# Gated cross-attention layer on one core: the first two projection jobs share one pass over half of the tokens

## The reference, cut to what matters

```python
x = x + tanh(g_xattn) * xattn(layernorm(x), ctx)      # x, ctx: 8 sequences x 128 tokens x 512
x = x + tanh(g_ffn)   * ffn(layernorm(x))

def xattn(hidden, ctx):            # H = 32 heads of DH = 128
    h_q = rmsnorm(hidden) @ w_q.T
    h_k = ctx @ w_k.T
    h_v = ctx @ w_v.T
    score = softmax(mask(h_q @ h_k.T + position_bias))
    return hidden + (score @ h_v) @ w_out.T
# ffn: a linear layer, a router over 15 entries and a low-rank update
```

## Time and profile before

| | |
|---|---|
| three runs | 832.13 us median (831.62 to 833.58) |
| the profiled execution | 832.1 us, span of the core 830.3 us |
| PE busy | 821.9 us (99%) |
| DVE busy | 491.8 us (59%) |
| ACT busy | 429.9 us (52%) |
| POOL busy | 348.3 us (42%) |
| the chain that ended last | 95% PE, 3% DVE, 1% DMA |
| PE's first instruction to first product of job 0 | 1.46 us to 6.75 us |
| `m1(2)` begins | 29.78 us |
| `m1(3)` begins | 36.66 us |

### The profile page before, as it was taken

One profiled execution on the slowest core, in us unless ns is written; L12 is line 12 of the kernel. 1 busy time (PEld: TensorE's weight loads), 2 busy tenths in 40 slices (PEclk: granted clock), 3 DMA queues, 4 the chain that ended last, 5 costly groups with the idle time before them and its releaser, 6 DMA issues.

```text
span 830.3 us, 13268 instructions
## 1 busy us (share of the span) xinstructions
PE 821.9 (99%) x4200; PEld 699.7 (84%) x4200; DVE 491.8 (59%) x919; ACT 429.9 (52%) x1065; POOL 348.3 (42%) x223
## 2 busy tenths in 40 slices
PE   8999999999999999999999999999999999999998
PEld 7888888888888888888888888888888888888876
DVE  6766666673353435555666565556655655677875
ACT  6667776676676665544444444444444444444320
POOL 0354544664556551434443344344434434432332
PEclk9999999999999999999999999999999999999999
DMA  8655555568555565766665566665666566655002
GB/s 307 199 170 151 163 158 153 165 183 268 173 163 161 173 201 161 241 193 195 188 190 193 190 198 203 203 202 177 187 193 175 178 191 188 216 166 160 32 26 77
DMA packets 147486, 147.60 MB, mean 178 GB/s; under 512 B 10992, under 2 KB 109936, under 8 KB 147056
## 3 DMA queue, kind: packets, MB, share of 16 engines
q1 hardware_dynamic: 147440, 147.02, 58.5%
HBM read 94.55 MB, written 52.43 MB: 177 GB/s over the span
## 4 chain that ended last, share of the span: by engine, by line
PE 95%; DVE 3%; DMA 1%; issue 1%; ACT 0%; SPq 0%; DVEq 0%
PE Sb L1528 7%; PE Ab L1539 7%; PE Sb L1359 7%; PE Sb L1361 7%; PE Sb L1360 7%; PE Vb L1350 4%; PE Vb L1351 4%; PE Vb L1352 4%; PE Kb L1350 4%; PE Kb L1351 4%; PE Kb L1352 4%; PE Ob L1350 4%; PE Ob L1351 4%; PE Ob L1352 4%; PE Ab L1361 3%; PE Ab L1359 3%
## 5 line engine op out<-in xcount | busy, mean ns | idle before, releaser
L536 POOL TENSOR_TENSOR bm<-bias,maskneg 128x512 f32<-128x512 f32 x64 | 83.6, 1306 | 178.6 <-DVE s_sb L1075 178.6
L756 ACT ACTIVATE p_exp<-s_sb,negmax 128x128 f32<-128x128 f32 x256 | 99.8, 391 | 76.5 <-DVE negmax L1077 76.5
L499 POOL TENSOR_TENSOR w_lo<-w_raw,w_hi 128x1280 fp32r<-128x1280 f32 (+1 forms) x29 | 87.0, 2999 | 116.4 <-ACT w_hi L626 116.4
L626 ACT ACTIVATE A_hi<-Ab 128x512 fp32r<-128x512 f32 x64 | 38.3, 598 | 164.0 <-PE Ab L1539 164.0
L1075 DVE TENSOR_TENSOR s_sb<-Sb,bm 128x512 f32<-128x512 f32 x62 | 42.8, 690 | 121.6 <-PE Sb L1528 121.6
L626 ACT ACTIVATE U<-Sb 128x512 f32<-128x512 f32 x90 | 53.9, 599 | 64.4 <-PE Sb L1361 64.0
L527 POOL TENSOR_TENSOR o_lo<-o_raw,o_hi 128x512 fp32r<-128x512 f32 x32 | 52.5, 1639 | 45.0 <-ACT o_hi L626 45.0
L626 ACT ACTIVATE w_hi<-w_raw 128x512 fp32r<-128x512 f32 (+3 forms) x68 | 60.1, 889 | 21.4 <-PE Kb L1361 8.2
L1539 PEld LDWEIGHTS Ab<-pT,V 128*128 128x128 f32 x512 | 66.9, 191 | 5.0
L1359 PE MATMUL Sb<-t_hi,w_lo 128*128 128x512 f32 x180 | 70.1, 389 | 0.0
L1361 PE MATMUL Sb<-t_hi,w_hi 128*128 128x512 f32 x180 | 70.0, 389 | 0.0
(11 more groups left out here) (278 smaller groups left out, 2099.7 us busy)
## 6 DMA issues: line engine op xcount, KB each, us to landing
qk_units<-unit_out SPq DMA_DIRECT2D x128, 256.0 KB, 2.9
qk<-qk_units SPq DMA_DIRECT2D x64, 512.0 KB, 4.8
p_rows<-p_blocks SPq DMA_DIRECT2D x64, 256.0 KB, 3.1
pT<-p_rows SPq DMA_DIRECT2D x256, 64.0 KB, 2.6
w_raw<-wqk SPq DMA_DIRECT2D x31, 512.0 KB, 4.1
v_raw<-wv SPq DMA_DIRECT2D x32, 256.0 KB, 4.1
o_raw<-wo SPq DMA_DIRECT2D x32, 256.0 KB, 3.9
stage<-ctxT SPq DMA_DIRECT2D x8, 256.0 KB, 5.8
```

The costliest lines, as they stand in the source:

```text
L499: pool.tensor_tensor(w_lo[:, n % 2, first:5, :], w_raw[:, n % 2, first:5, :], f32(w_hi[:, n % 2, first:5, :]), ALU.subtract).then_inc(w1_l ...
L536: pool.tensor_tensor(bm[:, :, :], bias4[:, q, :, :], maskneg[:, b:b + 1, :].broadcast_to([P, HU, S]), ALU.add).then_inc(bm_done, 1)
L626: act.activation(dst, src, ACT.Copy).then_inc(done, 1)
L756: last = act.activation(p_exp[:, i, :], s_sb[:, i, :], ACT.Exp, bias=negmax[:, i:i + 1], accum_out=rowsum[:, i:i + 1])
```

## The change

- The identity products go from 14 to 10.
- PE makes the first half of the tokens for jobs 0 and 1 together: for each context piece of B11 and B21, two units of job 0 and two of job 1 (`plain_together`). The second half of the tokens follows one unit after the other, job 0 and then job 1 (`plain_second`). The 96 matmuls are the same ones. `plain_done` counts finished units in the new order (`PLAIN_ORDER`): 1 and 2 are R11 and R21 of job 0, 3 and 4 those of job 1, 5 and 6 are R12 and R22 of job 0.
- The weights of job 1 come in two transfers between the first context pieces instead of one behind all pieces, and ACT and DVE split them there.
- On ACT the copies of units R11 and R21 of job 1 move from behind T4 to a place ahead of T3, and T1 and T2 move by a place or two.
- The load of the weights of job 2 waits for six splits of plain weights instead of four.

```diff
 PLAIN = 2
 
-WARM = 14
+WARM = 10
 
...
         plain_bank = [[X[0], Z[0], Ob[:, :], QP[:, :]], [X[1], Y, Z[1], Vb[:, :]]]
 
-        W0_SPLITS = (0, 4, 7)
+        PLAIN_ORDER = [(0, 0, 0), (0, 1, 0), (1, 0, 0), (1, 1, 0), (0, 0, 1), (0, 1, 1), (1, 0, 1), (1, 1, 1)]
+        PLAIN_ENDED = (6, 8)
+        W0_SPLIT = (6, 8)
+
+        def plain_count(n, i):
+            return PLAIN_ORDER.index((n, i % 2, i // 2)) + 1
 
...
-                    reached(sp, w0_lo, W0_SPLITS[n - 1])
+                    sp.wait_ge(w0_lo, W0_SPLIT[n - 2])
...
                     sp.dma_start(stage[:, k, c, :], ctxT[:, k, c, :]).then_inc(ld_c[k][c], 16)
-                if k == B11:
-                    sp.dma_start(w_raw[:, 0, A12, :], wqk[0, :, 1, :]).then_inc(ld_w0[1], 16)
-                    sp.dma_start(w_raw[:, 0, A22, :], wqk[0, :, 2, :]).then_inc(ld_w0[1], 16)
-            load_w(1)
+                    if k == B11 and c == 0:
+                        sp.dma_start(w_raw[:, 1, A11::A21, :], wqk[1, :, 0::3, :]).then_inc(ld_w1a, 16)
+                    if k == B11 and c == 1:
+                        sp.dma_start(w_raw[:, 0, A12, :], wqk[0, :, 1, :]).then_inc(ld_w0[1], 16)
+                        sp.dma_start(w_raw[:, 0, A22, :], wqk[0, :, 2, :]).then_inc(ld_w0[1], 16)
+                    if k == B21 and c == 0:
+                        sp.dma_start(w_raw[:, 1, A12:A21:A22 - A12, :], wqk[1, :, 1:3, :]).then_inc(ld_w[1], 16)
             load_w(2)
...
-            def start_hi(half):
-                act.wait_ge(ld_w0[half], 32)
+            def start_hi(n, half):
+                if n == 0:
+                    act.wait_ge(ld_w0[half], 32)
+                else:
+                    act.wait_ge((ld_w1a, ld_w[1])[half], 16)
                 for to, of in (((A11, A11), (S1, A21)), ((A12, A12), (A22, A22)))[half]:
-                    high(w_hi[:, 0, to, :], w_raw[:, 0, of, :], w0_hi)
-
-            def plain_first_hi(n):
-                act.wait_ge(ld_w[1], 16)
-                high(w_hi[:, n, A11:S1, :], w_raw[:, n, A11:S1, :], w0_hi)
-
-            def plain_last_hi(n):
-                high(w_hi[:, n, S1, :], w_raw[:, n, A21, :], w0_hi)
-                high(w_hi[:, n, A22, :], w_raw[:, n, A22, :], w0_hi)
+                    high(w_hi[:, n, to, :], w_raw[:, n, of, :], w0_hi)
 
...
-                    act.wait_ge(plain_done, 4 * (n - 1))
+                    act.wait_ge(plain_done, PLAIN_ENDED[n - 2])
...
             def plain_unit_out(i, n):
-                act.wait_ge(plain_done, 4 * n + i + 1)
+                act.wait_ge(plain_done, plain_count(n, i))
                 unit(i, n, plain_bank[n][i])
...
-            start_hi(0)
-            context_hi(B11, 0)
-            context_hi(B11, 1)
-            start_hi(1)
-            context_hi(B21, 0)
-            context_hi(B21, 1)
+            for half, k in enumerate((B11, B21)):
+                for c in range(2):
+                    start_hi(c, half)
+                    context_hi(k, c)
             for k in (B12, B22):
                 context_hi(k, 0)
                 context_hi(k, 1)
-            plain_first_hi(1)
-            plain_last_hi(1)
+            context_sum_hi(T1)
             plain_unit_out(R11, 0)
             plain_unit_out(R21, 0)
-            context_sum_hi(T1)
+            context_sum_hi(T2)
+            plain_unit_out(R11, 1)
+            plain_unit_out(R21, 1)
+            context_sum_hi(T3)
             plain_unit_out(R12, 0)
-            context_sum_hi(T2)
             first_weights_hi(2)
             plain_unit_out(R22, 0)
-            context_sum_hi(T3)
             last_weights_hi(2)
             context_sum_hi(T4)
-            plain_unit_out(R11, 1)
-            plain_unit_out(R21, 1)
             plain_unit_out(R12, 1)
...
-            def first_plain():
-
-                for half in range(2):
+            def plain_product(n, m, half, pair, c):
+                a, k, cols = ((A11, A12), (S1, A22))[m][pair], 2 * half + pair, slice(c * DH, (c + 1) * DH)
+                last = product(plain_bank[n][2 * half + m], w_hi[:, n, a, cols], w_lo[:, n, a, cols],
+                               c_hi[:, k, c, :], c_lo[:, k, c, :], pair == 0 and c == 0, pair == 1 and c == 1)
+                if pair == 1 and c == 1:
+                    last.then_inc(plain_done, 1)
+
+            def plain_together():
+
+                for pair in range(2):
+                    for c in range(2):
+                        pe.wait_ge(c_lo_done[pair], c + 1)
+                        for n in range(PLAIN):
+                            if c == 0:
+                                pe.wait_ge(w0_lo, 4 * pair + 2 * n + 2)
+                            for m in range(2):
+                                plain_product(n, m, 0, pair, c)
+
+            def plain_second(n):
+                for m in range(2):
                     for pair in range(2):
                         for c in range(2):
-                            k = 2 * half + pair
-                            if half == 0 and c == 0:
-                                pe.wait_ge(w0_lo, 2 * pair + 2)
-                            pe.wait_ge(c_lo_done[k], c + 1)
-                            cols = slice(c * DH, (c + 1) * DH)
-                            for m in range(2):
-                                a = ((A11, A12), (S1, A22))[m][pair]
-                                last = product(plain_bank[0][2 * half + m], w_hi[:, 0, a, cols], w_lo[:, 0, a, cols],
-                                               c_hi[:, k, c, :], c_lo[:, k, c, :], pair == 0 and c == 0,
-                                               pair == 1 and c == 1)
-                                if pair == 1 and c == 1:
-                                    last.then_inc(plain_done, 1)
-
-            def plain(n):
-
-                for i, (m, half) in enumerate(((0, 0), (1, 0), (0, 1), (1, 1))):
-                    if i == 0:
-                        pe.wait_ge(w0_lo, W0_SPLITS[n] + 1)
-                    if i == 1:
-                        pe.wait_ge(w0_lo, W0_SPLITS[n] + 3)
-                    for pair in range(2):
-                        a, k = ((A11, A12), (S1, A22))[m][pair], 2 * half + pair
-                        for c in range(2):
-                            cols = slice(c * DH, (c + 1) * DH)
-                            last = product(plain_bank[n][i], w_hi[:, n, a, cols], w_lo[:, n, a, cols],
-                                           c_hi[:, k, c, :], c_lo[:, k, c, :], pair == 0 and c == 0,
-                                           pair == 1 and c == 1)
-                    last.then_inc(plain_done, 1)
+                            if n == 0 and m == 0:
+                                pe.wait_ge(c_lo_done[2 + pair], c + 1)
+                            plain_product(n, m, 1, pair, c)
 
...
             warm_up()
-            first_plain()
-            for n in range(1, PLAIN):
-                plain(n)
+            plain_together()
+            for n in range(PLAIN):
+                plain_second(n)
             for n in range(PLAIN, JOBS):
                 m1(n)
```

More of the change, by code:

```diff
@@ L163, in build @@
         ld_w0 = [sem("ld_w0a"), sem("ld_w0b")]
+        ld_w1a = sem("ld_w1a")
         ld_w = [sem("ld_w0"), sem("ld_w1")]
@@ L927, in context_lo, with start_lo @@
                 low(c_lo[:, k, c, :], stage[:, k, c, :], c_hi[:, k, c, :], c_lo_done[k])
-            def start_lo(half):
+            def start_lo(n, half):
                 for i, (to, of) in enumerate((((A11, A11), (S1, A21)), ((A12, A12), (A22, A22)))[half]):
[L931 to L942, removed]
+                    dve.wait_ge(w0_hi, 4 * half + 2 * n + i + 1)
+                    low(w_lo[:, n, to, :], w_raw[:, n, of, :], w_hi[:, n, to, :], w0_lo)
             def context_sum(k, a, b, after):
@@ L1158, in step @@
                     y(0)
[L1160 to L1165, removed]
+            for half, k in enumerate((B11, B21)):
+                for c in range(2):
+                    start_lo(c, half)
+                    context_lo(k, c)
             for k in (B12, B22):
@@ L1168, in _ @@
                 context_lo(k, 1)
-            plain_first_lo(1)
-            plain_last_lo(1)
             context_sum(T1, B12, B11, 0)
```

## The result

| | median, us | runs |
|---|---|---|
| before | 832.03 | 8 (831.30 to 833.58) |
| changed | 834.24 | 8 (833.45 to 835.79) |

The ratio is 1.003, with a 95% interval of 1.002 to 1.004: slower by 2.2 us. The profiled execution took 833.91 us, with a span of 832.1, 1.8 us more than before. It is the second fastest of the changed kernel's eight executions.

What follows compares the result with a forecast made beforehand. PE, busy 99% of the span, sets the end, with m1(3) at 36.66 as the place to watch. The store wait and serial chain start m1(3) 2.3 us later: 832.1 + 2.3 = 834.4 us, range 832.4 to 835.7.

Steps and rivals of the forecast that it cites:

- PE's start: First product of job 0 on PE near 6.1 instead of 6.75, 0.6 us sooner; gap before 10.62 gone.
- the 1.75: On PE, m1(2) could begin at 28.0 instead of 29.78: 1.75 us, the most the change can bring.
- The store's landing: Store of job 0's R11, awaited by ACT's copy of job 1's R11, lands at 23.6, bounds 22.8 to 24.2.
- The serial chain: From the store through ACT, DVE and POOL: m1(3) begins at 38.95 instead of 36.66, 2.3 us later.
- L + 15.35: Start of m1(3) on PE if the first store lands at L; break-even at L = 21.3.
- The 1.0 us wait at `m1(2)`: PE waits 1.0 us for DVE's low parts of job 2's weights; m1(2) begins at 29.0.
- The sum: Whole kernel: 832.1 + 2.3 = 834.4 us; store bounds give 833.6 and 835.0.
- Stores in time: Rival: stores land by 21, job 0's last unit holds ACT, m1(3) at 35.7; 831.15 us, chance 0.10.
- DVE ahead of POOL: Rival: T4's sum goes before POOL's subtraction, chain 1.1 us shorter; 833.3 us, chance 0.10.
- The whole gain: Rival: stores in time and DVE ahead of POOL, so PE sets m1(3); 830.35 us, chance 0.04.
- More is lost: Rival: second store later, or late context piece or PE's lower pace exceeds the slack; 835.6 us and over, chance 0.10.
- the slack: At PE's start: up to 2.3 us worse changes nothing, since first_weights_hi(2) runs only at 26.1.

Runs made afterwards that it cites:

- x moved: Changed kernel, 2 MB load of x issued behind three stores and job 3's weights: 838.37 us; behind job 4's weights: 833.36 us, with 14 identity products 832.53 us.
- T4's sum first: Changed kernel with one wait added: POOL's 128x512 subtraction for job 2 waits for DVE's sum T4; 834.84 us.
- own buffers: Changed kernel in its own order, two more buffers so job 1's R11 and R21 copies wait for no store; 831.86 us.
- late copies, early sum and 14 identity products: Changed kernel, job 1's R11 and R21 copies behind T4's high part, T4's sum before job 2's low parts, 14 identity products; 830.98 us.
- 6 against 14 identity products: Changed kernel, job 1's R11 and R21 copies behind T4's high part, T4's sum before job 2's low parts: 833.0 us with 6, 830.98 with 14.
- x last: Changed kernel with the 2 MB load of x issued behind the load of job 4's weights, 10 identity products; 833.36 us.
- late copies: Changed kernel with ACT's copies of R11 and R21 of job 1 put back behind T4's high part; 831.86 us.
- late copies with early sum: Changed kernel, job 1's R11 and R21 copies behind T4's high part, T4's sum before job 2's low parts on DVE; 831.0 us.

## Why the prediction was right, step by step

- *PE's start*: forecast 6.1, measured 6.62. The first context piece landed later than before (its high part at 5.21 instead of 4.63), though the transfers ahead of it are the same ones. The term was too sharp: in the traces with this start and 10 identity products the first product came between 6.16 and 6.91. The gap at 10.6 went as forecast. PE's gain at `m1(2)` was 1.27 us, not what the 1.75 promised.
- *The store's landing*: forecast 23.6 with bounds of 22.8 and 24.2, measured 22.9 here and 23.4 with 14 identity products. Issued 2 us later, it landed 0.7 sooner: the queue ahead set it, as the runs with x moved show. The forecast's largest term was right. Its bounds just held in these two; in the run with T4's sum first, the same up to this point, the store landed at 22.6, outside them.
- *The serial chain*: forecast L + 15.35, measured 38.44 - 22.9 = 15.5. `first_weights_hi(2)` 26.1 forecast, 25.59 measured; POOL's start 1.35 us behind ACT's both times; the wait for `snapshot_1(2)` 1.5 forecast, 1.37 measured. The 1.0 us wait at `m1(2)` was not there as such: PE came half a microsecond later and DVE half a microsecond sooner.
- *The sum*: 834.4 forecast, 834.24 measured. By the profiled execution alone it is 1.8 us and not 2.3, for the store landed 0.7 sooner in it; the other executions lie higher on the whole, and no trace says why. So the mechanism is right, and that the numbers agree to 0.2 us is in part luck.
- *Stores in time*: priced at 831.15, measured 831.86 with own buffers. PE's start 0.4 us later (6.54 against 6.1) puts `m1(3)` at 36.10 and not at 35.7, which is more than half of the difference.
- *DVE ahead of POOL*: priced at 1.1 us, measured at nothing. The step that failed is "the chain is 1.1 us shorter": I moved the collision and counted it as gone.
- *The whole gain*: priced at 830.35; the nearest is 830.98, with late copies, early sum and 14 identity products, where PE's start is 0.75 us behind the forecast's. Not both conditions that I named were needed: T4's sum in DVE's idle time did it, with POOL and DVE still colliding later.
- *More is lost*: the slow start that I priced at some 2 us within the slack is real. Where the slack is gone it costs 1.7 us by `m1(3)` and 2.0 by the medians (6 against 14 identity products). That the changed kernel hides it is not shown, for no trace of it has a slow start. For it speaks that with x last a slow start let the 128x1280 high part begin at 25.30, ahead of the changed kernel's 25.59, and that the spans with 10 and with 14 identity products cover the same stretch (831.7 to 833.8 and 831.8 to 833.8).

## What to carry to other kernels

A copy out of PSUM that needs its staging buffer back waits for a store, and a store behind megabytes of loads takes two or three times its idle landing time and more (5.2 to 9.1 us here, against 2.6). Before such a copy is moved forward on an engine with a fixed order, look at when the earlier store lands and at what is queued behind the copy. Before a large load is moved to help a store, look at which stores come to stand behind it.

A shift of PE's early work is worth no more than what the slowest preparation chain of the next jobs allows. Find the idle time on the preparing engines and fill it, and the shift comes through.

## What the runs showed of the hardware

**DVE and POOL take turns.** POOL's 128x512 subtraction took 1.28 us alone and 1.52, 1.79 and 2.13 beside DVE; T4's sum 1.22 and 2.32; two low parts 2.43 and 3.44. The one that started second waited for the rest of the other's instruction and then ran. In the changed kernel DVE's low parts ended at 28.39, POOL's subtraction, begun at 28.02, at 29.54, and T4's sum, begun at 28.31, at 30.63: each 1.1 to 1.2 us behind the one before it. The Trainium skill (GPSIMD Engine Reference, its table of specifications) says that the two share SBUF interfaces, with contention for DVE instructions with two SBUF inputs. The traces agree, and add the size.

**PE's pace at the start.** After 6 identity products the first ten matmuls of 512 columns came every 0.43 us (the first 0.59), after 14 every 0.227, in all four traces that have 14. Of the eight traces with 10, one has the slow start and seven don't. The idle time ahead of the first product doesn't tell them apart: it was 0.81 us in the slow one, 0.99 in the changed kernel and 0.80 in the kernel before with 10. The column of the granted clock shows 1.00 for the slow stretches too, so here the pace is the better witness. In the middle of the program the column does show it, 0.50 after PE's wait of 4.17 us. 0.43 us for 512 columns is 1.2 GHz, 0.227 is near 2.4. The rows go with the Trainium skill (TensorE: Matmul & The Clock Gate, Back-to-back issue gap), which gives columns over 1.2 for the lower level.

**Executions that take longer.** By their spans, 3 of 11, 3 of 11 and 3 of 12 executions with 10 identity products (late copies, own buffers, late copies with early sum) lie 1.4 to 2.1 us over the median. With 14 they are rarer, not absent: none of 11, 1 of 11, 1 of 12, and 2 of 35 of the kernel before. That the lower pace at the start is their cause is not shown: it was seen in two profiled executions of other kernels, not in those themselves.

**Time outside the span.** In all 34 executions of the experiments with 14 identity products the execution's own time was 1.7 to 1.9 us longer than the span. With 10 it was 2.2 to 2.9 us longer in 13 of 77, and with 6 it was 2.5 to 2.8 in 4 of 11. So a shorter warm-up seems to cost up to 1 us now and then that no row of the profile shows. The cause is open.
